# Attention's prologue: values projected during the copies of the keys, query and key copies in turns, five row halves ahead of the first exponentials

## The reference

```python
x = x + _L0_conv_ref(_gn(x), ...)
x = x + _L1_conv_ref(_gn(x), L1_conv_qkv_w, L1_conv_qkv_b, ...)
x = x + _L2_conv_ref(_gn(x), ...)
x = x + _L3_conv_ref(_gn(x), L3_conv_w_qkv, L3_conv_b_qkv, ...)
```

```python
qkv = jnp.einsum('oc,bct->bot', qkv_w, xf) + qkv_b[None, :, None]
...
scores = jnp.einsum('bthe,bThe->bhtT', q, k) / jnp.sqrt(jnp.float32(EMB))
attn = jax.nn.softmax(scores, axis=-1)
out = jnp.einsum('bhtT,bThe->bthe', attn, v)
```

## Time and profile before

| | us |
|---|---|
| median of three runs | 5450.79 |
| lowest, highest | 5448.55, 5455.45 |
| the profiled execution | 5446.39 |
| its span in the trace | 5444.70 |
| TensorE busy | 4337.0 (80%) |
| VectorE busy | 3605.7 (66%) |
| ScalarE busy | 2146.4 (39%) |
| GpSimd busy | 2006.2 (37%) |

### The profile page before, as it was taken

One profiled execution on the slowest core, in us unless ns is written; L12 is line 12 of the kernel. 1 busy time (PEld: TensorE's weight loads), 2 busy tenths in 40 slices (PEclk: granted clock), 3 DMA queues, 4 the chain that ended last, 5 costly groups with the idle time before them and its releaser, 6 DMA issues.

```text
span 5444.7 us, 46953 instructions
## 1 busy us (share of the span) xinstructions
PE 4337.0 (80%) x17546; PEld 1966.3 (36%) x17546; DVE 3605.7 (66%) x4793; ACT 2146.4 (39%) x2639; POOL 2006.2 (37%) x681
## 2 busy tenths in 40 slices
PE   5688966889668896688866888668886698966988
PEld 2244422443224432244322443224432244322443
DVE  7764777636776477764677646876468664686746
ACT  4233452334423354243542435424254242542425
POOL 3531535405344053440534505445054450543504
PEclk7799977999779997799977999779997799977999
DMA  0020100210002100021000220001200012001120
GB/s 36 1 55 20 28 8 5 51 31 17 8 8 48 33 15 8 9 47 42 6 8 10 46 46 2 8 17 39 47 1 8 24 32 47 1 8 26 22 47 9
DMA packets 62965, 125.90 MB, mean 23 GB/s; under 512 B 18825, under 2 KB 21001, under 8 KB 62482
## 3 DMA queue, kind: packets, MB, share of 16 engines
q1 hardware_dynamic: 62738, 122.91, 9.7%
HBM read 12.23 MB, written 8.39 MB: 4 GB/s over the span
## 4 chain that ended last, share of the span: by engine, by line
PE 48%; DVE 28%; issue 10%; ACT 6%; SPq 4%; POOL 2%; DMA 2%; DVEq 0%; ACTq 0%; POOLq 0%
DVE mx L954 10%; PE PS L1261 8%; PE PS L1303 8%; PE PS L1098 7%; PE PS L1351 6%; PE PS L1385 3%; DVE work L846 3%; DVE work L848 3%; PE PS L1157 3%; ACT PT L624 2%; PE PS L1195 2%; PE PS L1073 2%; SPq L290 2%; PE PS L1312 2%; SPq L299 1%
## 5 line engine op out<-in xcount | busy, mean ns | idle before, releaser
L954 DVE TENSOR_REDUCE mx<-PS 128x1 f32<-128x512 f32 x2048 | 1337.0, 686 | 427.8 <-PE PS L1261 424.1
L624 ACT ACTIVATE PT<-PS 128x1024 f32<-128x1024 f32 x1024 | 1006.1, 1023 | 696.1 <-PE PS L1351 672.6
L1261 PE MATMUL PS<-KS,QS 96*128 96x512 f32 x2048 | 899.9, 482 | 190.9 <-DMA KS<-piece 84.7
L408 POOL TENSOR_TENSOR piece<-PT 128x2048 f32<-128x2048 f32 x48 | 219.8, 4580 | 2132.6 <-ACT PT L624 2132.6
L408 POOL TENSOR_TENSOR piece<-piece,PT 128x2048 f32<-128x2048 f32 x192 | 877.6, 4571 | 59.9 <-ACT PT L624 48.6
L388 POOL TENSOR_TENSOR work<-work,Crep 128x1024 f32<-128x1024 f32 x256 | 615.8, 2407 | 391.4 <-DVE work L846 192.4
L1351 PE MATMUL PS<-QS,KS 98*128 98x512 f32 x2048 | 682.4, 425 | 47.3 <-DMA QS<-nm 24.3
L1261 PEld LDWEIGHTS PS<-KS,QS 96*128 96x128 f32 x2048 | 379.2, 198 | 811.8 <-DVE mx L954 570.4
L1195 PE MATMUL PS<-dstk,sel 128*128 128x512 f32 (+1 forms) x640 | 316.3, 569 | 322.0 <-DVE work L848 132.7
L1303 PE MATMUL PS<-PT,Vt 128*32 128x512 f32 x4096 | 549.2, 608 | 27.3 <-ACT PT L624 27.3
L542 ACT ACTIVATE PS<-PS,Aneg 128x1024 f32<-128x1024 f32 x256 | 278.3, 1087 | 627.4 <-PE PS L1195 596.8
(11 more groups left out here) (200 smaller groups left out, 5230.5 us busy)
## 6 DMA issues: line engine op xcount, KB each, us to landing
QS<-piece SPq DMA_DIRECT2D x384, 128.0 KB, 2.4
KS<-piece SPq DMA_DIRECT2D x384, 128.0 KB, 2.4
xin<-x SPq DMA_DIRECT2D x8, 1024.0 KB
out<-xr SPq DMA_DIRECT2D x8, 1024.0 KB, 4.0
W<-wpack SPq DMA_DIRECT2D x2, 1024.0 KB
QS<-nm SPq DMA_DIRECT2D x128, 8.0 KB, 1.9
W<-wpack SPq DMA_DIRECT2D x1, 576.0 KB
W<-wpack SPq DMA_DIRECT2D x2, 256.0 KB
```

The source lines that it names most:

```text
L408: pool.tensor_tensor(total, first, PT[:, i % 3, :, :], ALU.add).then_inc(sum_pool.sem, 1)
L624: act.activation(PT[:, i % 3, 2 * pr:2 * pr + 2, :], PS[:, 2 + 2 * pr:4 + 2 * pr, :], ACT.Exp, scale=SCALE).then_inc(p_sb.sem, 1)
L954: dve.tensor_reduce(mx[:, at, cc:cc + 1], PS[:, row_slot(n, cc), :], AX.X, ALU.max).then_inc(r_max.sem, 1)
L1261: pe.matmul(PS[:, row_slot(n, cc), :], QS[0:kd, c, h, q * P:q * P + P], KS[0:kd, h, cc * N:cc * N + N], start=True, stop=True).then_inc(r_ ...
```

## The change

The values are projected directly after the queries of group 1, into banks 4 to 7, and copied by ScalarE ahead of its group 1 pieces. TensorE then waits, before rows 0 and 1, until the value copy has emptied the two banks that the row is going to use. The keys of group 1 are projected after rows 1 and 3. In VectorE's order the rest of group 1's queries stands after row 4 and that of the keys after row 8. SyncE issues two heads of queries ahead of the first keys of group 0 and then one head of each in turn; for group 1 all queries come first. In the wait for the first phase's maxima TensorE issues five row halves where it issued two.

```diff
-AHEAD = 3
+Q_REST_AFTER, K_REST_AFTER = 4, 8
+ROWS_AT_TURN = 5
...
+                    ahead = (2, GH)[g]
                     sp.wait_ge(*qk_rest(b, n + 1))
-                    for j in range(AHEAD):
+                    for j in range(ahead):
                         queries(j)
...
-                        if j + AHEAD < GH:
-                            queries(j + AHEAD)
+                        if j + ahead < GH:
+                            queries(j + ahead)
...
                 for g in range(GROUPS):
+                    for q in range(2 if g == 1 else 0):
+                        act.wait_ge(*v_ps(b, 2 * a + q + 1))
+                        act.activation(Vt[:, 4 * q:4 * q + 4, :].rearrange("p k c -> p (k c)"),
+                                       PS[:, 4 + 2 * q:6 + 2 * q, :].rearrange("p a n -> p (a n)"),
+                                       ACT.Copy).then_inc(v_sb.sem, 1)
...
-                for q in range(2):
-                    act.wait_ge(*v_ps(b, 2 * a + q + 1))
-                    act.activation(Vt[:, 4 * q:4 * q + 4, :].rearrange("p k c -> p (k c)"),
-                                   PS[:, 2 * q:2 * q + 2, :].rearrange("p a n -> p (a n)"), ACT.Copy).then_inc(v_sb.sem, 1)
...
-                rest(1, 0)
                 for n in range(PHASE_ROWS):
                     for cc in range(NC):
                         row_max(n, cc)
-                    if n == 2:
+                    if n == Q_REST_AFTER:
+                        rest(1, 0)
+                    if n == K_REST_AFTER:
                         rest(1, 1)
...
-                        ins = pe.matmul(PS[:, tt // 2, (tt % 2) * C:(tt % 2) * C + C], X[:, k, tt * P:tt * P + P],
+                        ins = pe.matmul(PS[:, 4 + tt // 2, (tt % 2) * C:(tt % 2) * C + C], X[:, k, tt * P:tt * P + P],
...
+                    if n < ahead and cc == 0 and ph == 0:
+                        pe.wait_ge(*v_sb(b, 2 * a + n + 1))
...
+                for tt in range(KT):
+                    project_v(tt)
 
                 for n in range(PHASE_ROWS):
                     for cc in range(NC):
                         row_scores(n, cc)
-                    if n < NC:
-                        if n == 0:
+                    if n in (1, 3):
+                        if n == 1:
                             pe.wait_ge(*qk_rest(b, 4 * a + 2))
-                        project_qk(1, 1, n)
-                    elif n < NC + KT:
-                        if n - NC in (0, 4):
-                            pe.wait_ge(*qk_rest(b, 4 * a + 3 + (n - NC) // 4))
-                        project_v(n - NC)
+                        project_qk(1, 1, n // 2)
                 turn_max(0)
-                pe.wait_ge(*v_sb(b, 2 * a + 2))
...
-                                next_rows(NC)
+                                next_rows(ROWS_AT_TURN)
```

## The result

| | before | after |
|---|---|---|
| median of nine runs | 5452.89 | 5465.42 |
| lowest, highest | 5448.55, 5455.45 | 5462.33, 5473.64 |
| the profiled execution | 5446.39 | 5467.21 |
| its span | 5444.70 | 5465.40 |

The ratio is 1.0027, with a 95% interval of 1.0017 to 1.0037: the changed kernel is slower by 12.5 us where 72 less were forecast. The profiled execution of before was faster than all nine of its timed runs, so the two traces lie 20.8 apart and not 12.5.

A forecast was written before the change was run, and what follows sets the result against it. Bound: each of 16 calls' prologue, waiting for head 0's keys and query copies, then VectorE's maxima. 16 x 5.2 (83), less 16 x 0.95 (15), plus 3.7: 72 us off 5446.4, so 5374; range 5346 to 5404.

The forecast's parts named there:

- the values ahead of row 0: Prologue: value matmuls take 3.4 us on TensorE, fill the gap before the keys land, and cost nothing.
- The turn: Wait for the first phase's maxima: five row halves delay the first product with the values, 0.95 us lost a call.
- SyncE's new wait: Maxima's copies wait 0 to 1.1 us for SyncE to finish group 1's copies; the extra halves hide it.
- Nothing else changes: After the sum: all 16 calls are on the chain and phases 1 to 3 keep their order; no further term.
- copies earlier: Prologue: head 0's keys become copies 7 to 9 and land at 296.4, where TensorE had started on them at 298.27.
- rests behind maxima: VectorE's order: a wait of 0.45 us at the first rest, none at the second.
- maxima at 0.60: Rows: VectorE's 32 halves take 19.2 us, not slowed by the array's clock falling to 0.5.
- the landing hidden: Turn: the maxima's landing is no longer last, giving back late landings of four calls, together 3.7 us.
- the four signs of being wrong: VectorE idle at second rest, late maxima copies, clock 1.00 at first scores, or over 0.62 for a maximum.
- the late copies of the maxima: Sign of being wrong: the maxima's copies issued later than 1.3 us after the joined maxima.
- Rival 1: TensorE's clock also stays up through rows and turn: 110 us gained, 5341 us; 12% chance.
- Rival 3: Slower: SyncE's 24 group 1 copies delay the maxima's copies; a loss from 0.92 us a copy, 5500 at 1.05; 3%.

The follow-up runs named there:

- v_split: The changed kernel with four value tiles projected ahead of row 0 and the other four after rows 6 to 9; 5416.67 us, ratio 0.9938.
- before_turn5: The kernel before with only the five row halves in the turn added; 5476.72 us, ratio 1.0055.
- warm0: The changed kernel with two dummy matmuls between second and third pair of scores in phase 0's first step; 5445.34 us, ratio 0.9986.
- warm3: The changed kernel with dummy matmuls in phase 3, six in the first step and two in the second; 5450.60 us, ratio 1.0002.
- kept_warm3: kept_warm2 with three more dummy matmuls in phase 3's first step; 5341.39 us, ratio 0.9794 to the kernel before.
- split_turn2_warm3: v_split with two row halves in the turn instead of five, plus warm3's dummy matmuls in phase 3; 5394.67 us, ratio 0.9892.
- split_oldcopies: v_split with SyncE's old order of copies restored; 5421.09 us, ratio 0.9939 to the kernel before.
- kept_warm2: v_split with two halves in the turn, plus dummies: one behind each half of rows 11 to 15, four behind the transpose, seven behind the turn's halves; 5360.98 us.

## Why the prediction was wrong

**The step that failed first** is "Sixteen value matmuls at 0.85 for four are 3.4", in the part on the values ahead of row 0. The count and the row came from two different views. The program's order lists 16 value matmuls in a call; the trace lists 32, since each of these fp32 matmuls is there twice: the row "x4" at 0.85 stood for one tile of two matmuls and not for two tiles. It is no factor that holds for every row: row halves and scores, whose operands are tiles of type fp32r, are listed once (2048 row halves on the page, 32 x 4 x 16 in the program). It should have been 8 tiles x 0.85 = 6.8; measured are 7.07. Half of that filled the gap, as forecast, and the other half stood behind it: row 0 came at 13.4 and not 10.1, and of the 5.2 forecast to the joined maxima 4.1 were missing. v_split, which removes the surplus, puts row 0 at 10.4 and the joined maxima at 33.6. The forecast said 33.0. Row 0 has 0.25 of the rest. The other 0.4 are TensorE's projections after rows 1 and 3, of 1.88 each, which the sum left out: VectorE waits 0.68 and 0.17 behind them, where one wait of 0.45 was foreseen at the rest.

**The turn** was the term that was sized right: 0.95 foreseen; 0.8 lost to the first product with the values in the change, and the same in before_turn5. The first score started 3.84 after the issue in most calls, foreseen was 3.8. The agreement at the product is in part luck: it came 8.87 after the issue in most calls and not 8.4, as the clock was still low, but before it had come at 8.1 in the mean and not at the 7.49 of the call that the sum took. SyncE's new wait came in three of the 16 calls (the maxima's copies issued at 38.95 to 39.31 instead of 38.34) and was hidden by the halves, as said: the first score comes 5.10 or 5.11 behind the joined maxima in 14 calls, these three among them, and 5.16 and 5.19 in the other two. But the sum ended at the first product with the values. It took "Nothing else changes" for granted behind it, and that is **the second step that failed**. Behind it lie 1.0 to phase 1 and 1.25 in phase 3, both the clock's. warm0 shows the first by giving it back with two dummies; warm3 shows the second in the same way. Rows 5 had a hint: TensorE had no idle time between the first scores before, and the prediction itself said that ScalarE becomes the bound there once the halves are gone. It priced that wait and not what the idle time does to the clock.

**How much each step weighs.** The forecast for the profiled execution was 5374 and it took 5467, a miss of 93 us. The joined maxima are 66 of it (4.1 in each of 16 calls), the turn 2, the stretch to phase 1 15, and phase 3 20; the stretches between calls and the earlier first call take off 10.

**What was right:** copies earlier, rests behind maxima (VectorE had no idle time at the second rest), maxima at 0.60 with the clock at 0.50 (14 in 8.45), the landing hidden. Of the four signs of being wrong only one came, the late copies of the maxima in three calls, and there it cost nothing; none of them looked at the start of row 0, though the first maximum, forecast at 8.2 after the first copy, was there to be checked, and none looked behind the first product. Rival 1, that the clock stays up, did not happen by itself. kept_warm3 brings it about with dummies, and its first product with the values comes 5.95 earlier than before, where rival 1 had 6.9. That both end at 5341 is luck: the kernel of kept_warm3 has other halves in the turn and its values in two parts, and gains in phase 3 too. By the Trainium skill, TensorE: Matmul & The Clock Gate, HAM oscillation — how this bites in real kernels, a kernel should leave TensorE no long idle gaps. That rule would have had the change gain by closing its long gap. In the traces here the clock no longer fell at that gap, yet it was low for longer in a call (25.0 instead of 17.9), because it fell earlier in the row stretch, and the 0.26 that the change left behind the first scores cost what warm0 gives back. Rival 3 put the loss in SyncE's queue, where it was not.

The sum with the terms as measured, from the traces: -1.06 to the joined maxima, +0.8 for the turn, +1.0, +1.25, -0.6 between the calls: +1.4 a call. What stays open is that last term. Between 162.8 and 164.5 pass from a call's last exponential to the next call, through code that is the same in all these kernels, and two executions of one kernel differ by 0.7 of it; the 0.6 is no more than that. Open too is what decides whether the clock falls in phase 3.

## What to carry to other kernels

Count instructions and durations in the same view: an order that lists a matmul once and a trace that lists it twice differ by a factor of two, and a gap that is filled twice over is a new bound. Work that is moved out from between an engine's waits leaves idle time behind, and on TensorE that idle time has a price of its own, in the clock of stages far from the edit. Where TensorE waits anyway, a few dummy matmuls that fit the idle time are cheap to try (20 us of 5465 in one place here), but ones that do not fit, or stand where the clock was up, cost about as much as they might have given (15 to 17 us in split_turn2_warm3).

## What the runs showed of the hardware

The same phase 3, instruction for instruction, took 16.5 to 16.6 in every call with the clock at 1.00 and 17.8 to 19.6 in every call in which it fell. Which of the two it was changed with edits that shift a call by 1 to 2 us: 16 falls of 16 in v_split, one in split_oldcopies. The low clock between the first score and the first product with the values cost 1.8 a call (5.5 against 3.7). A dummy matmul of 128 columns in fp32 is listed twice and took 0.117 for each entry at the full clock, with its weight load in the same rhythm (28 in 3.29). Row halves of about 0.2 us, one every 0.60, did not hold the full clock in any call of the eleven runs whose rows have no dummies. With one dummy behind each of the last ten halves it held through rows and turn in 25 of 32 calls (kept_warm2 and kept_warm3).
